# The ninth layer of a twelve-layer kernel: expert weights loaded whole, the second product in row tiles, two experts a step, turns without copies

## What is computed

```
DM, NEXPERTS, SETS, ESIZE = (128, 32, 4, 32)
grouped = x.reshape(b, s // g, g, d)                     # g = 32
logits = jnp.einsum('bntd,des->bntes', grouped, Wc) + bc
logits = logits + tie
perm = (logits == jnp.max(logits, axis=-3, keepdims=True)).astype(x.dtype)
permuted = jnp.einsum('bntd,bntes->bnesd', grouped, perm)
inner = jax.nn.relu(jnp.einsum('bnesd,esdf->bnesf', permuted, W1) + b1)
result_permuted = jnp.einsum('bnesf,esdf->bnesd', inner, W2) + b2
result = jnp.einsum('bnesd,bntes->bntd', result_permuted, perm)
```

## Time and profile before

| | us |
|---|---|
| median of three runs | 3195.32 (3193.84 to 3203.55) |
| the profiled execution | 3200.41 |
| its span | 3198.4 |
| of it the ninth layer, 1580.3 to 1686.2 | 105.9 |

### The profile page before, as it was taken

How to read it: one execution, slowest core, us unless ns; L and a number is a source line. 1 busy time by engine, 2 the same in 40 slices (tenths; PEclk the granted TensorE clock), 3 DMA queues, 4 the chain that set the end, 5 groups by cost and what they waited for, 6 DMA issues and landing times.

```text
span 3198.4 us, 64562 instructions
## 1 busy us (share of the span) xinstructions
PE 2903.5 (91%) x24081; PEld 1875.2 (59%) x24081; DVE 1790.1 (56%) x5797; ACT 1345.5 (42%) x3664; POOL 690.9 (22%) x1543
## 2 busy tenths in 40 slices
PE   8999988887899987999678997869999999999898
PEld 7888865566457765666446775534444444444465
DVE  6777766665246667656866665753333333333544
ACT  5565553332248862236576885421111121121221
POOL 3444430000037750014204664100000000000000
PEclk9999999998899997997788998979999999999999
DMA  4111110000011110030122113030000000000000
GB/s 131 47 47 47 47 29 1 1 1 1 4 43 48 47 42 3 23 89 3 19 40 62 39 39 139 3 128 3 1 1 1 1 1 1 1 1 1 1 1 14
DMA packets 159389, 91.86 MB, mean 29 GB/s; under 512 B 74787, under 2 KB 156326, under 8 KB 157990
## 3 DMA queue, kind: packets, MB, share of 16 engines
q1 hardware_dynamic: 159078, 87.74, 10.1%
HBM read 84.02 MB, written 3.67 MB: 27 GB/s over the span
## 4 chain that ended last, share of the span: by engine, by line
PE 52%; DVE 8%; issue 5%; POOL 4%; ACT 3%; DVEq 2%; POOLq 1%; ACTq 0%
PE banks L3341 23%; POOL probs L1210 3%; PE banks L920 2%; PE banks L3757 2%; PE banks L3748 2%; PE banks L3746 2%; PE banks L1651 2%; PE banks L901 1%; POOLq L1211 1%; PE banks L3402 1%; PE banks L929 1%; ACT inner L3124 1%; PE banks L888 1%; PE banks L2259 1%; PE banks L1889 1%
## 5 line engine op out<-in xcount | busy, mean ns | idle before, releaser
L1010 ACT ACTIVATE probs<-probs,nbias 128x257 f32<-128x257 f32 x512 | 254.8, 507 | 0.0
L1210 POOL TENSOR_SCALAR probs<-probs,rinv 128x257 f32<-128x257 f32 x512 | 236.9, 482 | 30.0 <-DVE rinv L1104 26.6
L3341 PE MATMUL banks<-Wn,hT 128*64 128x512 f32 x1024 | 226.7, 595 | 0.0
L3341 PE MATMUL banks<-Wz,hT 128*64 128x256 f32 x2048 | 226.4, 379 | 0.0
L3341 PE MATMUL banks<-Wr,hT 128*64 128x512 f32 x1024 | 225.2, 592 | 0.0
L3607 POOL COPY rb<-hT 128x512 f32<-128x512 f32 x32 | 35.9, 1122 | 823.4 <-ACT hT L3414 798.3
L3341 PEld LDWEIGHTS banks<-Wz,hT 128*64 128x64 f32 x2048 | 147.1, 137 | 87.6 <-issue 18.3
L3581 DVE TENSOR_TENSOR pr<-hb,banks 128x512 f32<-128x512 f32 x32 | 22.0, 688 | 298.0 <-PE banks L3396 298.0
L714 POOL TENSOR_SCALAR probs<-probs,rinv 128x257 f32<-128x257 f32 x256 | 120.1, 482 | 202.3 <-DVE rinv L654 201.7
L3341 PEld LDWEIGHTS banks<-Wr,hT 128*64 128x64 f32 x1024 | 73.7, 137 | 132.4 <-issue 127.8
L3341 PEld LDWEIGHTS banks<-Wn,hT 128*64 128x64 f32 x1024 | 70.8, 137 | 132.8 <-issue 129.5
(11 more groups left out here) (638 smaller groups left out, 6693.3 us busy)
## 6 DMA issues: line engine op xcount, KB each, us to landing
kvT<-in_ctx_T SPq DMA_DIRECT2D x192, 128.5 KB
kv<-in_ctx SPq DMA_DIRECT2D x64, 128.0 KB
kv<-in_ctx SPq DMA_DIRECT2D x32, 256.0 KB
W<-in_L_ffn_W SPq DMA_DIRECT2D x64, 64.0 KB, 2.1
Wr<-in_L_ffn_w_hh_T SPq DMA_DIRECT2D x1, 4096.0 KB
Wn<-in_L_ffn_w_hh_T SPq DMA_DIRECT2D x1, 4096.0 KB
Wz<-in_L_ffn_w_hh_T SPq DMA_DIRECT2D x1, 4096.0 KB
v_last<-v_last SPq DMA_DIRECT2D x192, 8.0 KB, 1.6
```

What stands on the lines that cost most here:

```text
L1010: i = e.activation(s, s, ACT.Exp, bias=self.nbias[v][:, r:r + 1], scale=self.scale, accum_out=self.rows_sum[v][:, r:r + 1])
L1210: e.tensor_scalar(s, s, self.rinv[v][:, r:r + 1], 1.0, ALU.mult, ALU.mult)
L3341: mm = e.matmul(self.bank[b][hf * BATCH:(hf + 1) * BATCH, 0:n], lhs, rhs, start=start, stop=stop, tile_position=(0, hf * BATCH))
```

## The change

All of W1 and W2 is loaded with the stage's weights, in an order that the host makes, W2 already with the inner dimension on partitions; so the ring of eight, its transfers, the turn of W2 and its copy go. A step takes two experts. ScalarE rectifies all 128 partitions of an expert at once. The second product is four matmuls of 32 rows an expert, each set from its own 32 partitions, into banks 4 to 7, and VectorE adds b2 while it takes both experts out of the four banks. In the way back the slices of G are turned directly, without Rb, and ScalarE copies the result to rb. In the routing bc and the tie are added in one operation, and ScalarE takes three of the four gathered banks. GpSimd and SyncE have no work of their own left in this stage.

```diff
-        self.b2 = self.weight("b2", [P, P], whole, w["b2"].rearrange("e s d -> (e s) d"))
+        self.b2 = self.weight("b2", [P, ES], whole, w["b2_T"])
+        self.W1 = self.weight("W1", [P, E * P], whole, w["W1_T"])
+        self.W2 = self.weight("W2", [P, E * P], whole, w["W2_T"])
...
+        for n, phase in self.staggered(self.PAIRS, (2, 0), 2):
             if phase == 0:
...
+                self.inner_pe(e, n)
             if phase == 2:
...
+                self.expert_pe(e, n)
+        self.G_back.wait_ge(e, self.PAIRS)
+        for t, phase in self.staggered(NT, (2, 0), 2):
...
                 for b in range(BPT):
-                    i = e.transpose(bank[z][:, b * P:(b + 1) * P], self.Rb[r][:, b * P:(b + 1) * P], p.ident[:, :])
+                    i = e.transpose(bank[z][:, b * P:(b + 1) * P], self.G3[:, :, 4 * t + b], p.ident[:, :])
                 i.then_inc(self.R_turned.up(), 1)
...
+    def inner_pe(self, e, n):
+        self.inner_ready.wait_ge(e, n - 1)
+        for k in range(2):
+            x = 2 * n + k
+            for s in range(self.SETS):
+                i = e.matmul(self.bank[n % 2][32 * s:32 * s + 32, k * BATCH:(k + 1) * BATCH], self.W1[:, x * P + 32 * s:x * P + 32 * s + 32],
+                             self.G[:, x * 256 + s * BATCH:x * 256 + (s + 1) * BATCH], start=True, stop=True, tile_position=(0, 32 * s))
+        i.then_inc(self.inner_mm.up(), 1)
+
+    def expert_pe(self, e, n):
+        self.inner_ready.wait_ge(e, n + 1)
+        self.G_back.wait_ge(e, n)
+        for k in range(2):
+            x = 2 * n + k
+            for s in range(self.SETS):
+                rows = slice(32 * s, 32 * s + 32)
+                i = e.matmul(self.bank[4 + s][:, k * BATCH:(k + 1) * BATCH], self.W2[rows, x * P:(x + 1) * P],
+                             self.inner[n % 4][rows, k * BATCH:(k + 1) * BATCH], start=True, stop=True)
+        i.then_inc(self.expert_mm.up(), 1)
...
     def act(self, e):
...
-                for b in (1, 3):
+                for b in (1, 2, 3):
                     for s in range(4):
                         i = e.copy(self.G3[:, :, 16 * g + 4 * s + b], bank[2 + b][:, s * P:(s + 1) * P])
                 i.then_inc(self.G_act.up(), 1)
...
+        for n in range(self.PAIRS):
+            self.inner_mm.wait_ge(e, n + 1)
+            self.expert_mm.wait_ge(e, n - 3)
+            for k in range(2):
+                at = slice(k * BATCH, (k + 1) * BATCH)
+                i = e.activation(self.inner[n % 4][:, at], bank[n % 2][:, at], ACT.Relu, bias=self.b1[:, 2 * n + k:2 * n + k + 1])
             i.then_inc(self.inner_ready.up(), 1)
...
         for t in range(NT):
-            self.R_turned.wait_ge(e, t - 3)
-            for b in (2, 3):
-                i = e.copy(self.Rb[t % 4][:, b * P:(b + 1) * P], self.G3[:, :, 4 * t + b])
-            i.then_inc(self.Rb_act.up(), 1)
-            if t == NT - 2:
+            self.R_turned.wait_ge(e, t + 1)
+            self.spread_mm.wait_ge(e, t - 3)
+            e.copy(self.rb[t % 4][:, :], bank[t % 2][:, :]).then_inc(self.rb_ready.up(), 1)
+            if t == 11:
                 self.next_root(e, 0)
                 self.next_root(e, 1)
-        self.next_root(e, 2)
+            if t == 14:
+                self.next_root(e, 2)
 
     def dve(self, e):
...
-                e.tensor_scalar(lg[:, :], bank[0][:, :], self.bc[:, 0:1], None, ALU.add).then_inc(self.logit_ready.up(), 1)
-                e.drain()
-                e.tensor_tensor(b32(lg[:, :]), b32(lg[:, :]), self.tie[:, :].unsqueeze(1).to_broadcast([P, 16, SEQ]), ALU.add)
+                e.scalar_tensor_tensor(b32(lg[:, :]), b32(bank[0][:, :]), self.bc[:, 0:1], self.tie[:, :].unsqueeze(1).to_broadcast([P, 16, SEQ]),
+                                       ALU.add, ALU.add).then_inc(self.logit_ready.up(), 1)
                 e.drain()
...
+        of_sets = self.prog.banks[:, 4 * 512:8 * 512].rearrange("p (s c) -> p s c", s=4)[:, :, 0:2 * BATCH].rearrange("p s (k b) -> p k s b", k=2)
+        for n in range(self.PAIRS):
+            self.expert_mm.wait_ge(e, n + 1)
+            e.tensor_tensor(self.G[:, n * 512:(n + 1) * 512].rearrange("p (k s b) -> p k s b", k=2, s=4), of_sets,
+                            self.b2[:, 8 * n:8 * n + 8].rearrange("p (k s) -> p k s", k=2).unsqueeze(3).to_broadcast([P, 2, 4, BATCH]),
+                            ALU.add).then_inc(self.G_back.up(), 1)
...
+    out["L2_ffn_W1_T"] = w["L2_ffn_W1"].transpose(2, 0, 1, 3).reshape(P, -1)
+    out["L2_ffn_W2_T"] = w["L2_ffn_W2"].transpose(1, 3, 0, 2).reshape(P, -1)
+    out["L2_ffn_b2_T"] = w["L2_ffn_b2"].transpose(2, 0, 1).reshape(P, -1)
```

More of the change, by code:

```diff
@@ L3001 @@
 class L2Ffn(Stage):
-    E, SETS, F, RING = 32, 4, 32, 8
+    E, SETS, F, PAIRS = 32, 4, 32, 16
     ES = E * SETS
@@ L3008, in __init__ @@
         super().__init__(prog, prefix)
-        w, sb, sig, E, ES, RING = self.w, self.sb, self.sig, self.E, self.ES, self.RING
+        w, sb, sig, E, ES, PAIRS = self.w, self.sb, self.sig, self.E, self.ES, self.PAIRS
         whole = lambda t: t[:, :]
@@ L3041, in pe @@
     def pe(self, e):
-        p, bank, RING = self.prog, self.bank, self.RING
+        p, bank = self.prog, self.bank
         self.norm_pe(e)
@@ L3067, in pe @@
         self.G_act.wait_ge(e, 4)
-        for x, phase in self.staggered(self.E, (2, 0), 2):
-            d, z = x % RING, x % 2
+        for n, phase in self.staggered(self.PAIRS, (2, 0), 2):
             if phase == 0:
[L3071 to L3078, removed]
-            if phase == 2:
[L3080 to L3084, removed]
+                self.inner_pe(e, n)
+            if phase == 2:
+                self.expert_pe(e, n)
+        self.G_back.wait_ge(e, self.PAIRS)
+        for t, phase in self.staggered(NT, (2, 0), 2):
             z, r = t % 2, t % 4
[L3086 to L3089, removed]
+            if phase == 0:
                 self.rb_ready.wait_ge(e, t - 1)
                 for b in range(BPT):
-                    i = e.transpose(bank[z][:, b * P:(b + 1) * P], self.Rb[r][:, b * P:(b + 1) * P], p.ident[:, :])
+                    i = e.transpose(bank[z][:, b * P:(b + 1) * P], self.G3[:, :, 4 * t + b], p.ident[:, :])
                 i.then_inc(self.R_turned.up(), 1)
-            if phase == 3:
+            if phase == 2:
                 self.rb_ready.wait_ge(e, t + 1)
@@ L3156, in dve @@
                 self.gather_mm.wait_ge(e, g + 1)
-                for b in (0, 2):
-                    for s in range(4):
-                        i = e.tensor_copy(self.G3[:, :, 16 * g + 4 * s + b], bank[2 + b][:, s * P:(s + 1) * P])
+                for s in range(4):
+                    i = e.tensor_copy(self.G3[:, :, 16 * g + 4 * s], bank[2][:, s * P:(s + 1) * P])
                 i.then_inc(self.G_dve.up(), 1)
[L3161 to L3164, removed]
-                self.expert_mm.wait_ge(e, x - RING + 1)
-                e.tensor_copy(self.W2T[d][:, :], bank[z][:, 0:P]).then_inc(self.W2T_ready.up(), 1)
-            if phase == 2:
-                self.expert_mm.wait_ge(e, x + 1)
-                e.tensor_copy(self.G[:, x * 256:(x + 1) * 256], bank[4 + z][:, 0:256]).then_inc(self.G_back.up(), 1)
@@ new lines, in dve @@
+        for n in range(self.PAIRS):
[3 more added lines that the diff above has]
+                            ALU.add).then_inc(self.G_back.up(), 1)
+        for t in range(NT):
+            x = X[:, t * P:(t + 1) * P]
+            self.spread_mm.wait_ge(e, t + 1)
+            e.tensor_tensor(x, x, bank[2 + t % 2][:, 0:P], ALU.add).then_inc(self.x_done.up(), 1)
+            if t % 4 == 3 and t < 12:
+                e.drain()
+                self.next_statistics(e, t // 4)
+            if t >= NT - 4 and t < NT - 1:
+                self.next_rows(e, t - NT + 4)
```

73 lines of the change are left out of this document (11 added, 62 removed).

## The result

The changed kernel takes 3181.9 us in the median (3200.8 for the kernel before, measured beside it), a ratio of 0.994 with a 95% interval of 0.9925 to 0.9955: 14 to 24 us less. The profiled execution took 3180.66 us, with a span of 3178.9.

The account below looks back on a forecast made before the run. Bounds: ScalarE's activations in the experts, a VectorE chain in routing, VectorE on the way back. Routing -1.0, experts -17.5, way back -7.2 make -25.7: 3200.4 to 3174.7, less 5.1 for the median, 3169.6; range 3161 to 3187.

Parts of the forecast that it names:

- so I take the middle, 1.62: Experts: time of a pair in us, between 1.45 at full clock and 1.8 at half; 27.4 us against 44.9, -17.5.
- a pair over 2 us: Experts: sign that the prediction is wrong; it expected 1.4 to 1.8 us from second product to second product.
- its sum for 1.2 GHz, 1.8: Experts: us of a pair at half clock, from product, add and hand-overs, with the product at 0.95.
- I take nothing: Way back: no cost for turns reading G strided as stationary operand; 20.5 us against 27.7, -7.2.
- Rival (a): Way back: strided turns at VectorE's rate, 133 ns a load, 25.9 us instead of 20.5; kernel 3175; chance 0.15.
- the two steps at half clock: Way back: two tile steps at half clock add 1.3 us (2 x 0.65), giving 20.5 us.
- Three groups at 0.3: Routing: three groups gain 0.3 us each, -0.9 of the part's -1.0.
- (b): Clock stays at 1.2 GHz: experts 31.1 us, way back 27.6, total -14.9, kernel 3180; chance 0.12.
- (c): Experts: row tiles don't overlap, 73 ns an instruction, pair 2.25, part 37.5 us; kernel 3180; chance 0.06.
- (d): Way back: strided turns at ScalarE's rate, total -5.5, kernel 3190, no measurable change; chance 0.07.
- (e): Way back: strided turns dearer still, at 3 ns a column 56.9 us, kernel slower at 3206; chance 0.05.
- Weights at nothing: Weight loads issued when the eighth layer starts, 144 us ahead: covered, cost 0; without cover up to 53 us wait.

Follow-up runs that it names:

- e1: Changed kernel plus one idle full-array 128x256 matmul behind each pair of first products; ratio 0.998 to the kernel before, stage 101.6 us.
- e4: Changed kernel with second product and add in units of two sets over three pairs of banks; ratio 0.9924 to the kernel before, stage 82.1 us.
- e7: Changed kernel plus an idle full-array 128x512 matmul behind each pair of first products; one run, 3179.0 us, stage 89.3 us.
- e12: e1 with its idle matmul widened to 128x512 in the first four pairs alone; ratio 0.993 to the kernel before, stage 85.3 us.
- e2: Changed kernel with the second product streaming 128 columns instead of 64 behind the same 16 loads; one run, 3182.2 us, stage 89.4 us.
- e5: Changed kernel with the routing's 16 copies of G back to 8 on VectorE and 8 on ScalarE; ratio 0.9938 to the kernel before, stage 85.0 us.
- e11: Changed kernel with e4's units, e5's copies, e3's contiguous turns and e9's add walk; 3170.8 us, ratio 0.9909 to the kernel before.
- e3: Changed kernel with adds writing a second tile in turn order, so turns read contiguous columns; ratio 0.9955 to the kernel before, stage 92.2 us.
- e9: e3 with the add walking column, expert, set, so eight values are written in a row; ratio 0.9947 to the kernel before, stage 86.4 us.

## Why the forecast held in direction, and where its terms were off

It said 3169.6; 3181.9 came, 12.3 us more: inside the range of 3161 to 3187, but outside the forecast's own 3163 to 3176. Of the 12.3, 6.0 are its sum, -19.7 instead of -25.7. Another 5.4 is the base: it started from 3195.3, and the kernel before took 3200.8 beside the changed one. Its ranking was right: the experts give most, then the way back, then the routing; ScalarE leaves the experts' chain; no wait for weights appears.

**Experts, -11.3 for -17.5.** The step that failed is "so I take the middle, 1.62". It rested on the busy share: 81% had gone with a clock of 1.00. The changed part has 27.36 of 33.60 us busy, also 81%, and a clock of 0.50. What the share doesn't tell is how much of the array works: before, a pair had four 128x256 instructions of a full 128x128 array and two full turns of W2; after, only tiles of 32 rows or 32 columns. e1 and e4 show that being busy isn't enough, e7 that more full-array work raises the clock, e12 that it then holds with less of it. Of the 0.41 us that a pair is dearer, 0.18 is the clock taken in the middle (1.8 against 1.62), 0.18 the product (1.13 against 0.95), and the hand-overs 0.05 (about 0.20 for 0.16). Times 16 that is 6.5 us; the run-up to the first product gave 0.4 back. By the prediction's own sign, a pair over 2 us, this part was wrong; even its sum for 1.2 GHz, 1.8, lies under the 2.03. The product was sized by columns between two neighbours, while e2 shows that columns hardly count, and its 16 loads take 0.97 us. At full clock the sum was near: 0.6 foreseen, 0.67 measured in e7 and e12, so an estimate of 1.52 for 1.45. The low level was there when the experts began: the clock fell at 1616.2 (above), behind a stretch in which TensorE mostly waited for ScalarE's copies, and the small tiles didn't raise it again in 33.6 us, nor in e4 without gaps. Whether they would hold 2.4 GHz once there isn't shown: only e5 and e11 entered at 1.00, and there it fell 1.0 us later, after a wait of 2.6 us; e12 still has its 256 wasted columns. Which feature of the full matmuls counts, rows, columns in a row or their share of the time, stays open.

**Way back, -5.3 for -7.2.** The failed step is "I take nothing" for the strided operand. Rival (a) had the mechanism, at 133 ns a load and a pitch of 1.43; measured are 99 ns (0.79 us from turn to spread over eight) and 1.14. e3 and e9 show that it is the stride: without it the turn is back at 0.66 us. About 12 tiles at full clock make 2.3 us, against the 1.9 by which the part was missed; the two steps at half clock were as foreseen.

**Routing, -3.3 for -1.0.** The loop was right in its members (copies 2.84 to 3.03, pick copy 0.58 to 0.64, gather 1.17), and mis-sized in two terms. "Three groups at 0.3" set 5.7 against 5.98 for each group. From gather to gather it was 5.97, 5.86 and 5.08 us before (the 5.98 holds for the first alone) and 5.48, 4.75 and 4.71 after: 2.0 less and not 0.9. And the last gather, at 2.4 GHz (1.17 us) where before it took 2.09, gave 0.9 for which no term stood. The start (-1.1 for -0.85) and the tail (+0.7 for +0.8) were right. The fused operation costs 752 ns, as the plain one. Moving the copies to ScalarE was itself a loss of about 2 us, by e5: what this part gains comes from the fused add and the clock.

**Rivals.** (b) was half true: experts at 1.2 GHz, and with 33.6 us beyond its bound of 31.1, as the product was dearer; the way back wasn't at 1.2. That its 3180 lies next to the result is luck: it has 27.6 us for the way back (22.4 came), and a base that was 5.4 too low. (c) fails by e7: 16 instructions in 0.60 us at full clock, 38 ns each and not 73. (d) and (e) fail by the turn's 0.85 us. **Weights at nothing** held: the windows row gives a DMA share of 0.01 in the experts, 0.50 before, and the eighth layer, into which the transfers moved, took 146.4 us against 144.5, but 143.1 to 144.4 with the same transfers in e1 to e5: no cost shows.

## What to carry to other kernels

Cutting a full-array matmul into small tiles removes work, but it can also remove what would raise the clock to 2.4 GHz. Look at the clock with which the stretch begins, too. Read the granted clock of the stretch beside its busy share, and price each new step at both levels; taking the middle is right for neither. Where row tiles replace a wide matmul, price the loads before the streamed columns. When a tile is read across by one engine and written by another, put the scatter into runs of two or more values on the writing side, and see which engine has slack. And when two engines hand one set of banks back and forth, try splitting it into a ring: here it took 0.37 us off a pair of 2.03 at an unchanged clock.

## What the runs showed of the hardware

- The clock has a memory: the same loop ran at 1.2 GHz through all its pairs in e1 and at 2.4 GHz in e12, after four pairs with a 128x512 filling.
- Useless work can pay for itself through the clock: 128x512 in each pair left the pair at 2.02 us instead of 2.03, at 2.4 GHz instead of 1.2.
- A 32x128 load costs 61 ns in a row of 16 over four row groups at 1.2 GHz; a 128x128 operand with 256 bytes between columns costs 24 ns a load more at 2.4 GHz and about 4 at 1.2 (a turn of eight 1.15 us against 1.12).
- VectorE's add of 512 columns takes 692 ns with eight values of 4 bytes in a row on the writing side and 1022 with single ones 512 bytes apart; stepping 2 KB at a time through PSUM on the reading side costs nothing.
